# A long convolution's forward Fourier transform: one product over 112 rows against two over 57 and 56 rows of folded sums and differences

## The reference, cut to what matters

```python
# sublayer 1: a state-space layer (B=16, L=112, H=512)
xz = einsum('bld,ed->bel', hidden_states, W_in)
x, z = split(xz, 2, axis=1)                     # 512 channels each
x = silu(conv1d(pad(x), conv_w, depthwise) + conv_b)   # 4 taps, causal
k = _s4d_kernel(...)                            # (512, L), real
n = 2 * L
y = irfft(rfft(x, n=n) * rfft(k, n=n), n=n)[..., :L]
y = (y + x * D) * silu(z)
out = einsum('bhl,dh->bld', y, W_out)
# x1 = layernorm(x + out); sublayer 2 adds x1's projection and a gathered,
# decayed context (layernorm again); sublayer 3 is a mixture of 8 experts,
# one expert for each token (layernorm again)
```

## Time and profile before

| | us |
|---|---|
| median of three runs | 395.71 |
| span of the profiled execution | 390.5 |
| what lies around the span (median less span) | 5.2 |
| stage A, from VectorE's first tap to its last | 25.6 to 60.3 |
| turning point from A to B | 60.3 to 91.5 |
| stage B, steps 3 to 15 | 91.5 to 208.8 |
| stage B, the last steps, and routing | 208.8 to 245 |
| stage F, experts | 245 to 390 |

### The profile page before, as it was taken

The page is one execution under the profiler, slowest core; times in us unless marked ns, Lnnn a source line. Parts: engine busy times, 40 slices in busy tenths (PEclk is TensorE's granted clock), DMA queues, the critical chain, the costliest instruction groups (busy, mean ns, idle before and its releaser), DMA issues.

```text
span 390.5 us, 7319 instructions
## 1 busy us (share of the span) xinstructions
PE 333.8 (85%) x2035; PEld 276.7 (71%) x2036; DVE 249.4 (64%) x491; ACT 124.3 (32%) x332; POOL 225.8 (58%) x390
## 2 busy tenths in 40 slices
PE   2549996789999999999999532799999999999990
PEld 1225544668888887888888422699999999999970
DVE  6997999976887777777776648323443443443431
ACT  2437883541122222222222100144324324334220
POOL 5958994075776767676556502415456556555553
PEclk9957996899999999999999975799999999999996
DMA  7800000243354444444445046401100101001110
GB/s 227 298 0 1 1 0 3 60 136 117 95 155 158 129 151 147 147 134 128 128 128 166 12 176 280 161 2 42 39 29 22 45 27 40 28 20 40 37 37 24
DMA packets 17025, 34.84 MB, mean 89 GB/s; under 512 B 3456, under 2 KB 8455, under 8 KB 16360
## 3 DMA queue, kind: packets, MB, share of 16 engines
q1 hardware_dynamic: 14840, 29.88, 23.8%
q0 software_dynamic: 1872, 4.59, 4.1%
q10 hardware_dynamic: 288, 0.07, 0.1%
HBM read 30.86 MB, written 4.20 MB: 90 GB/s over the span
## 4 chain that ended last, share of the span: by engine, by line
PE 75%; DVE 12%; POOL 4%; issue 4%; ACT 2%; DMA 1%; DVEq 0%; POOLq 0%; ACTq 0%
PE ps L1331 17%; PE ps L1349 15%; PE ps L1200 7%; PE ps L1263 7%; PE ps L1245 6%; PE ps L1147 4%; PE ps L1190 4%; PE ps L1191 4%; PE ps L1283 3%; DVE w L888 2%; DVE w L873 2%; PE ps L1155 1%; PE ps L1287 1%; PE ps L1318 1%; POOL stage_b L583 1%
## 5 line engine op out<-in xcount | busy, mean ns | idle before, releaser
L1331 PEld LDWEIGHTS ps<-stage_b 128*128 128x128 f32 x576 | 68.4, 195 | 2.6 <-DVE stage_b L1096 1.0
L1331 PE MATMUL ps<-stage_b 128*128 128x128 f32 x576 | 68.8, 279 | 1.2 <-ACT stage_b L820 1.2
L1349 PE MATMUL ps<-w,stage_b 128*128 x288 | 65.2, 380 | 0.6 <-DVE stage_b L1121 0.6
L1349 PEld LDWEIGHTS ps<-w,stage_b 128*128 128x128 f32 x288 | 53.3, 190 | 7.5 <-issue 1.0
L603 POOL TENSOR_TENSOR stage_b<-stage_b 112x512 f32<-112x512 f32 x16 | 21.6, 1350 | 42.3 <-DVE stage_b L942 21.7
L925 DVE TENSOR_SCALAR stage_b<-stage_b 112x256 f32<-112x256 f32 (+1 forms) x50 | 20.5, 411 | 35.5 <-POOL stage_b L671 21.8
L811 ACT ACTIVATE stage_b<-ps,b 128x128 f32<-128x128 f32 x144 | 39.2, 384 | 7.2 <-issue 7.2
L942 DVE TENSOR_TENSOR stage_b<-ps,w 112x512 f32<-112x512 f32 x64 | 39.7, 682 | 2.6 <-PE ps L1191 1.3
L643 POOL DMA_INDIRECT stage_b<-x_rows,stage_b x21 | 34.3, 1633 | 10.0 <-issue 6.0
L1200 PEld LDWEIGHTS ps<-w 128*128 128x128 f32 x256 | 32.9, 202 | 8.2 <-issue 6.9
L1096 DVE COPY stage_b<-w 128x2048 f32 x19 | 23.5, 1241 | 19.6 <-issue 14.0
(11 more groups left out here) (156 smaller groups left out, 536.7 us busy)
## 6 DMA issues: line engine op xcount, KB each, us to landing
w<-in_w SPq DMA_DIRECT2D x16, 512.0 KB, 3.9
w<-in_w SPq DMA_DIRECT2D x16, 256.0 KB, 2.9
w<-in_w SPq DMA_DIRECT2D x4, 1024.0 KB, 8.2
stage_b<-in_ctx SPq DMA_DIRECT2D x16, 224.0 KB, 2.9
w<-in_x_t SPq DMA_DIRECT2D x4, 448.0 KB, 5.3
stage_b<-in_x SPq DMA_DIRECT2D x16, 112.0 KB, 2.9
x_rows<-stage_b SPq DMA_DIRECT2D x16, 112.0 KB, 1.9
w<-in_w_in SPq DMA_DIRECT2D x2, 512.0 KB, 6.4
```

What stands on the lines that cost most here:

```text
L1331: last_ = m.matmul(ps[:, 2 * par + f // 4, (f % 4) * P:(f % 4 + 1) * P], w1_now[par][:, k, f * P:(f + 1) * P], rows_t[:, par, k * P:(k + 1 ...
L1349: last_ = m.matmul(ps[:, 4 + par, 0:D], h_t[:, par, f * P:(f + 1) * P], w2[:, e, f, :], start=(f == 0), stop=(f == FT - 1))
```

## The change

Time steps t and 112-t meet the same cosine and the opposite sine, up to a sign that is fixed for even and for odd frequencies. So VectorE makes, for every unit, the sums x[t] + x[112-t] (57 of them) and the differences x[t] - x[112-t] (56 of them), with x[112] taken as zero. They are laid at places 0 to 56 and 64 to 119 (`ODD` = 64, `BINS` = 120) of `folded`, and it is `folded` that TensorE turns. The transform is then one product of rows 0 to 56 and one of rows 64 to 119, both against 120 columns of the constant `fold`, and both again over 512 moving columns. Bank 0 receives the real parts of even frequencies and the imaginary parts of odd ones, bank 1 the others; places 57 to 63 are padding.

Around it: `spec` has four tables of 120 rows for three of 112 (one more product in `kernel_spectrum`, a wider copy L761), and is a tensor of its own. `prod`, `y_spec` and the inverse transform have 120 rows for 112. `turn_kernel` uses bank 3 instead of bank 4. GpSimd clears two small strips at the start. TensorE's turn now waits for `fold_set` instead of `act_x`, and ScalarE's SiLU waits for `fold_set` instead of `xt_ps`. TensorE's 20 steps of stage B are written out instead of partly looped; the other engines keep their loops.

```diff
+HF = L // 2
+ODD = 64
+BINS = ODD + HF
...
-        x_time = r.cut(NB * H, L).rearrange("p (b h) -> p b h", b=NB)
+        x_time = r.cut(NB * H, BINS).rearrange("p (b h) -> p b h", b=NB)
...
@@ GpSimd
+            g.memset(conv_x[:, :, :, L:L + 1], 0.0)
+            g.memset(folded[:, :, :, HF + 1:ODD], 0.0).then_inc(edge_set, 1)
...
@@ ScalarE, a_silu
-                need(act, xt_ps, unit - 1)
-                a.activation(conv_x[:, par, :], conv_acc[:, par, :], ACT.Silu, bias=conv_b[:, h:h + 1])\
+                need(act, fold_set, unit - 1)
+                a.activation(conv_x[:, par, :, 0:L], conv_acc[:, par, :].rearrange("p (b t) -> p b t", b=CB),
+                             ACT.Silu, bias=conv_b[:, h:h + 1])\
...
-                a.activation(spec[:, :, tile], ps[0:L, 5:8, tile], ACT.Copy).then_inc(spec_set, 1)
+                a.activation(spec[:, :, tile], ps[0:BINS, 4:8, tile], ACT.Copy).then_inc(spec_set, 1)
@@ VectorE
+            def a_fold(unit, h):
+
+                x_now, to = conv_x[:, h % 2], folded[:, h % 2]
+                dve.wait_ge(act_x, unit + 1)
+                need(dve, xt_ps, unit - 1)
+                v.tensor_tensor(to[:, :, 0:HF + 1], x_now[:, :, 0:HF + 1], x_now[:, :, L:HF - 1:-1], ALU.add)
+                v.tensor_tensor(to[:, :, ODD:], x_now[:, :, 0:HF], x_now[:, :, L:HF:-1], ALU.subtract)\
+                 .then_inc(fold_set, 1)
...
+            dve.wait_ge(edge_set, 1)
             for h in range(HT):
                 a_step(0, h)
+                if h > 0:
+                    a_fold(h - 1, h - 1)
             with dve.Fori(1, NC) as c:
                 for h in range(HT):
                     a_step(c, h)
+                    a_fold(HT * c + h - 1, (h - 1) % HT)
+            a_fold(HT * NC - 1, HT - 1)
...
-                    for n, (x_part, k_part) in enumerate(((0, 0), (1, 1), (0, 1), (1, 2))):
-                        last = v.tensor_tensor(prod[:, n, :], ps[0:L, x_part, :], spec[:, k_part, :], ALU.mult)
+                    for n in range(4):
+                        last = v.tensor_tensor(prod[:, n, :], ps[0:BINS, n % 2, :], spec[:, n, :], ALU.mult)
@@ TensorE
             def a_turn(unit, h):
-                pe.wait_ge(act_x, unit + 1)
+                pe.wait_ge(fold_set, unit + 1)
                 need(pe, xt_set, unit - 1)
                 for b in range(CB):
-                    last_ = m.transpose(ps[0:L, 4 + h % 2, b * P:(b + 1) * P],
-                                        conv_x[:, h % 2, b * L:(b + 1) * L], ident)
+                    last_ = m.transpose(ps[0:BINS, 4 + h % 2, b * P:(b + 1) * P], folded[:, h % 2, b, :], ident)
...
-                    m.matmul(ps[0:L, 0, :], const("f_re", L), x_time[:, b, :], start=True, stop=True)
-                    m.matmul(ps[0:L, 1, :], const("f_im", L), x_time[:, b, :], start=True, stop=True)\
+                    m.matmul(ps[0:BINS, 0, :], const("fold")[0:HF + 1], x_time[0:HF + 1, b, :], start=True, stop=True)
+                    m.matmul(ps[0:BINS, 1, :], const("fold")[ODD:BINS], x_time[ODD:BINS, b, :], start=True, stop=True)\
...
-                m.transpose(ps[0:L, 4, h * P:(h + 1) * P], kern[:, h, :], ident).then_inc(kern_ps, 1)
+                m.transpose(ps[0:L, 3, h * P:(h + 1) * P], kern[:, h, :], ident).then_inc(kern_ps, 1)
...
-                for s, name in enumerate(("f_re", "f_im0", "f_d")):
-                    last = m.matmul(ps[0:L, 5 + s, tile], const(name, L), kern_t[:, tile], start=True, stop=True)
+                for s, name in enumerate(("k_a", "k_b", "k_c", "k_d")):
+                    last = m.matmul(ps[0:BINS, 4 + s, tile], const(name, L), kern_t[:, tile], start=True, stop=True)
...
-            b_steps(pe, step)
+            for s in range(NB + EPI):
+                step(s // 2, s % 2)
```

More of the change, by code:

```diff
@@ L71, in constant_columns, with bins @@
     put("eps", np.full((P, 1), EPS))
-    angle = 2 * np.pi * np.outer(t, t) / NFFT
-    cos, sin = np.cos(angle), np.sin(angle)
-    nyquist = (-1.0) ** t
-    zero0 = (t > 0).astype(float)
-    put("f_re", cos)
-    f_im = -sin
-    f_im[:, 0] = nyquist
-    put("f_im", f_im)
-    put("f_im0", -sin * zero0)
-    f_d = cos.copy()
-    f_d[:, 0] = nyquist
-    put("f_d", f_d)
-    g_re = 2 * cos / NFFT
-    g_re[0] = 1.0 / NFFT
+    even, odd = 2 * np.arange(HF + 1), 2 * np.arange(HF) + 1
+    def bins(n, f_even, f_odd):
+        a = np.zeros((n, BINS))
+        angle = 2 * np.pi * np.arange(n)[:, None] / NFFT
+        a[:, :HF + 1] = f_even(angle * even)
+        a[:, ODD:] = f_odd(angle * odd)
+        return a
+    minus_sin = lambda v: -np.sin(v)
+    fold = np.zeros((BINS, BINS))
+    fold[:HF + 1] = bins(HF + 1, np.cos, minus_sin)
+    fold[HF] *= 0.5
+    fold[ODD:] = bins(HF, minus_sin, np.cos)
+    put("fold", fold)
+    for name, f_even, f_odd in (("k_a", np.cos, np.sin), ("k_b", np.sin, np.cos),
+                                ("k_c", minus_sin, np.cos), ("k_d", np.cos, minus_sin)):
+        put(name, bins(L, f_even, f_odd))
+    g_re, g_im = 2 / NFFT * bins(L, np.cos, np.cos).T, -2 / NFFT * bins(L, np.sin, np.sin).T
+    g_re[[0, HF]] *= 0.5
     put("g_re", g_re)
-    g_im = -2 * sin / NFFT
-    g_im[0] = nyquist / NFFT
     put("g_im", g_im)
@@ L180, in decoder_layer @@
         conv_acc = r.cut(2 * CW).rearrange("p (r n) -> p r n", r=2)
-        conv_x = r.cut(2 * CW).rearrange("p (r n) -> p r n", r=2)
+        conv_x = r.cut(2 * CB * (L + 1)).rearrange("p (r b t) -> p r b t", r=2, b=CB)
         n_hits = PT * T // 2
@@ L205, in decoder_layer @@
         w_out = r.cut(HT * D).rearrange("p (k d) -> p k d", k=HT)
-        spec = r.cut(3 * H, L).rearrange("p (s h) -> p s h", s=3)
+        folded = r.cut(2 * CB * BINS).rearrange("p (r b t) -> p r b t", r=2, b=CB)
+        spec = sb("spec", [BINS, 4 * H])[:, :].rearrange("p (s h) -> p s h", s=4)
         shared = sb("shared", [P, 2048])
@@ L220, in two @@
             return r.cut(2 * words, rows).rearrange("p (r n) -> p r n", r=2)
-        prod = r.cut(4 * H, L).rearrange("p (s h) -> p s h", s=4)
-        y_spec = r.cut(2 * H, L).rearrange("p (s h) -> p s h", s=2)
+        prod = r.cut(4 * H, BINS).rearrange("p (s h) -> p s h", s=4)
+        y_spec = r.cut(2 * H, BINS).rearrange("p (s h) -> p s h", s=2)
         z_act, gated = two(HT * L), two(HT * L)
@@ L282, in decoder_layer @@
         kern_ps, kern_sb, spec_ps, spec_set = (sem(s) for s in ("kern_ps", "kern_sb", "spec_ps", "spec_set"))
-        in_ps, acc_set, tap_set, conv_done, act_x, xt_ps, xt_set = (
-            sem(s) for s in ("in_ps", "acc_set", "tap_set", "conv_done", "act_x", "xt_ps", "xt_set"))
+        in_ps, acc_set, tap_set, conv_done, act_x, fold_set, edge_set, xt_ps, xt_set = (
+            sem(s) for s in ("in_ps", "acc_set", "tap_set", "conv_done", "act_x", "fold_set", "edge_set", "xt_ps",
+                             "xt_set"))
         dft_ps, prod_set, y_set, z_ps, z_set, idft_ps, gate_set, out_ps = (
@@ L602, in step @@
                     need(pool, idft_ps, b)
-                    g.tensor_tensor(y_spec[:, 0, :], prod[:, 0, :], prod[:, 1, :], ALU.subtract)
+                    g.tensor_tensor(y_spec[:, 0, :], prod[:, 0, :], prod[:, 1, :], ALU.add)
                     g.tensor_tensor(y_spec[:, 1, :], prod[:, 2, :], prod[:, 3, :], ALU.add).then_inc(y_set, 1)
@@ L720, in a_move @@
                 a.activation(x_time[:, bass.ds(CB * c, CB), h * P:(h + 1) * P],
-                             ps[0:L, 4 + h % 2, :].rearrange("p (b h) -> p b h", b=CB), ACT.Copy)\
+                             ps[0:BINS, 4 + h % 2, :].rearrange("p (b h) -> p b h", b=CB), ACT.Copy)\
                  .then_inc(xt_set, 1)
@@ L758, in _ @@
                 act.wait_ge(kern_ps, h + 1)
-                a.activation(kern_t[:, tile], ps[0:L, 4, tile], ACT.Copy).then_inc(kern_sb, 1)
+                a.activation(kern_t[:, tile], ps[0:L, 3, tile], ACT.Copy).then_inc(kern_sb, 1)
                 act.wait_ge(spec_ps, h + 1)
-                a.activation(spec[:, :, tile], ps[0:L, 5:8, tile], ACT.Copy).then_inc(spec_set, 1)
+                a.activation(spec[:, :, tile], ps[0:BINS, 4:8, tile], ACT.Copy).then_inc(spec_set, 1)
             def step(pair, q):
@@ L1245, in step @@
                             last_ = m.matmul(ps[:, 3, h * L:(h + 1) * L], y_spec[:, s, h * P:(h + 1) * P],
-                                             const(name, L), start=(s == 0), stop=(s == 1))
+                                             const(name, BINS), start=(s == 0), stop=(s == 1))
                     last_.then_inc(idft_ps, 1)
```

## The result

The changed kernel takes 406.03 us (median of 4 runs, 404.33 to 406.99), the kernel before in the same series 395.45 us. The ratio is 1.0257, 95% interval 1.0212 to 1.0302: slower, by 10.6 us. The forecast was 412.1 us in a range of 401 to 421.

What follows compares the result with a forecast made beforehand. VectorE was taken to bound stage A's last part and TensorE stage B. Stage A +19.4, the rest +0.5 and stage B -3.5 gave +16.4 us on the profiled execution, 412.1 us, in a range of 401 to 421.

Steps and rivals of the forecast that it cites:

- Part 1: Stage A, VectorE: the folds' own work, 0.32 us each, 0.64 a pair per unit, all on the path.
- Part 2: Stage A: VectorE's folds wait for GpSimd's instructions at the shared port, 1.68 us a pair in 9 units, 0.64 in three.
- Part 3: Edges of stage A: last unit's fold costs 1.4 us, units 0 to 3 cost 1.0; later SiLU wait costs nothing.
- Part 4: Stage B, two forward products on row tiles: 0.43 us overlap less 0.18 transitions, 0.25 a step, 14 steps, -3.5 us.
- Part 5: The rest: TensorE's written-out loop costs and gains nothing; the kernel's spectrum and step 0's transform together +0.5 us.
- port contended, tiles side by side: Rival: folds pay the port in stage A, stage B's products overlap fully; 403.6 us, chance 0.13.
- Free port: Rival: in stage A the port costs nothing for such short folds; 402.8 us, chance 0.17.
- one after the other: Rival: stage B's tiles don't overlap and pay both transitions, 0.18 us a step; 418.1 us, chance 0.12.
- faster: Rival: full overlap in stage B, 0.86 us a step, beside a free port decides; 394.3 us, chance 0.07.
- clock rival: Rival: TensorE, busy for half of stage A's units, falls to 1.2 GHz, +4.0 us; 416.1 us, chance 0.13.

Runs made afterwards that it cites:

- e7: Changed kernel with the folds' second input read from PSUM (folded values left out) and TensorE's turn a unit later: 399.16 us, ratio 1.011.
- e4: Changed kernel with the folds' second input read from PSUM instead of SBUF, folded values left out: 403.09 us, ratio 1.019.
- e6: Changed kernel with GpSimd's 28 products of 256 elements in stage A cut into 56 of 128: 406.54 us, ratio 1.028.
- e12: Changed kernel with TensorE's turn a unit later and the folds placed between the taps, GpSimd's products whole: 401.74 us, ratio 1.014.
- e5: Kernel before the change with only TensorE's loop of stage B written out: 395.67 us, ratio 0.9985.
- e3: Changed kernel with both forward products on rows 0 to 56, one tile, differences left out: step 9.38 us; total 412.19 us, not compared.
- e2: Changed kernel without folds, SiLU writing straight into `folded`, signal's transform left out: first reduction at 58.59 us; total 383.49 us, not compared.
- e1: Changed kernel with both forward products over all 120 rows, so no row tiles, same result: 414.14 us, ratio 1.044.
- e8: Changed kernel with folds' second input from PSUM (folded values left out), turn a unit later, folds between the taps: 401.15 us, ratio 1.016.
- e9: Changed kernel with GpSimd's products halved, the turn a unit later and the folds between the taps, result complete: 401.28 us, ratio 1.019.

## Why the prediction was right, and where it was off

**Direction and size.** Forecast +16.4 us, measured +12.0 on the spans and +10.6 on the medians. The bound engines were read rightly: VectorE in stage A pays, TensorE in stage B gains, and stage F keeps its length (143.7 us from the first expert product on, 143.8 before). The number lay in the range although one step was wrong: the range had been drawn to hold the rivals too, and the two errors below, some 2.4 us in stage A and 2.6 in stage B, both made the forecast too slow.

**Part 1, the folds' own work: right.** Records of 0.38 and 0.39 us where nothing contends, 0.59 a pair in e7 (2.60 less the taps' 2.01), for 0.64.

**Part 2, the port: right in kind, somewhat too dear.** Folds of 0.9 to 1.0 us beside GpSimd and 0.39 after it, units of 3.73 there (61.52 to 65.25) for 3.69 predicted. e4 and e6 show the cause: 8.3 us of the folds' time go when their second input leaves SBUF, and waits shrink with GpSimd's instruction. Too dear, because 8 units paid and not 9, at 3.47 us on the mean (37.50 to 65.25): up to 52 us several first folds found the port free. I had let the folds deny GpSimd 0.64 us a unit and so put its end near 68.7; the end moved from 62.9 to 65.07.

The Trainium skill (SBUF — State Buffer, Who interferes with whom) calls the pair of ports that VectorE and GpSimd share an exclusive lock, and says that a VectorE instruction with two SBUF inputs contends with a GpSimd instruction that reads SBUF. The traces agree: 0.38 us with an input in PSUM, 0.91 with both in SBUF. It doesn't foretell who is next when both wait. The folds and GpSimd's products took turns, and e12's gain rests on that; but e5's L912, with two SBUF inputs of one element each, waited for three products in a row (2.19 us for 0.16), so turns are not a rule.

**Part 3, the edges.** Units 0 to 3 cost 1.5 us (the fifth unit's first tap at 37.50 for 35.99), predicted 1.0. That they came near is luck: the idle 1.84 us that the prediction let the folds fill was a half-clock stretch of TensorE in that one execution, and in e5 the fifth unit starts at 34.33. The last unit cost 1.4 (73.87 to 77.32 less 2.01), as predicted. "SiLU now waits for a fold that is a whole unit older: nothing" held, but I missed its counterpart: TensorE's turn now waits for a fold where it had waited for SiLU, and `a_in` stands behind it. It cost at most 1.1 us in the changed kernel (0.48 of it before the fifth unit, with TensorE at half clock); in e4, without port waits over it, some 2.5 of the 4.5. By stages: 1.5 + 11.5 (eight units) + 2.5 (three) + 1.4, unrounded +17.0, predicted +19.4.

**Part 4, the tiles: the step that failed.** The prediction said: "If starts stay in order, only high1 and low2 can overlap: 0.43 us. I take that". They don't stay in the code's order. The second product's first MATMUL starts 0.01 us after the first product's first, so the four run as two pairs in 1.05 us. In e3, with the same calls in the same order but on one tile, both MATMULs of the first product start before those of the second (128.54 and 129.49), so it is the second tile that lets them pass. The predicted transition of 0.18 us was too low as well, e3 gives 0.29. So 0.85 - 0.29 = 0.56 a step instead of 0.25, and over the 12 steps -6.1 us for 12 x -0.25 = -3.0 (the first of them was shorter than 9.08 before). The range held it (up to 0.86). I had the rule of program order from the Trainium skill (TensorE: Matmul & The Clock Gate, Packing small matmuls). Its short distance between starts agrees with the rows, its order rule doesn't hold for the starts of two float32 products on two row tiles. The Trainium skill also says (TensorEngine Tiling (Array Packing), Key Properties) that a change of tiling mode drains the engine; e3's 0.29 us agree.

A second figure of Part 4: the followers could follow. VectorE has 88.01 of 102.20 us in stage B for 81.39 of 108.40, and TensorE isn't kept waiting. But it is near: of the changed kernel's chain of waits in these steps long parts run through GpSimd's L614, L594 and VectorE's L968 and L984, beside a TensorE without a gap.

**Part 5.** The loop is worth nothing (e5), as predicted. Between the reduction and step 3 the kernel takes 31.15 us for 31.08: the spectrum's +0.5 doesn't show. (e5 and e2 take 33.1 and 33.3, since their first reduction is early and waits for GpSimd.)

**The rivals.** The truest mechanism was one I gave 0.13: port contended, tiles side by side, 403.6 us. It undersold the transitions. "Free port" fell with e4, "one after the other" with e1, "faster" with both. The clock rival, at +4.0 us, fell by the windows: TensorE busy for 3.09 of 6 us and at 1.00. Only between 33 and 37 us did the clock fall again, and VectorE waited 0.48 us for it.

**What stays open.** How GpSimd and VectorE are ordered when both wait was read off timelines, not tried by itself, and L912's three lost turns are unexplained; so are the last steps' 1 to 2 us and the waits in e8. Whether folds on ScalarE or in TensorE's turning product would pay wasn't tried.

## What to carry to other kernels

A fold that halves TensorE's work for one stage is paid on another engine in another stage: price it where that engine is the bound. Here the folds alone cost more (16 x 0.59 us of VectorE; e7, without port waits, reaches step 3 8.4 us later than the kernel before, 1.2 of it its late first fold) than twelve overlapped steps bring (6.1 us). An instruction with two SBUF inputs on VectorE beside a busy GpSimd should stand behind one that reads PSUM, not behind its like: that alone was 4.3 us. And when a signal is moved to a later producer (turn after fold instead of after SiLU), follow the consumer's queue: what is issued behind it waits too. A wait in one profiled execution can be the clock's: look at the granted clock there before an edit is given the credit.

## What the runs showed of the hardware that I had not expected

- Two float32 products on different 64-row tiles interleave by halves: starts at 125.23, 125.24, 125.76, 125.77. A pair takes 0.53 us where one MATMUL of 512 columns alone takes 0.43. In e3 the first and the last of the four take 0.53 and 0.52 us and the two between them 0.43, so the excess stands at the way into the tile and out of it.
- Of two folds beside GpSimd the second waits 0.53 us (0.91 less 0.38) when it follows the first, and not behind a tap of 0.66 us, with GpSimd's products whole. With the halves it has 0.45 us on the mean behind a tap (e9).
- The turns aren't kept always: L912 in e5, 128x1 with both inputs in SBUF, took 2.19 us beside three whole products of GpSimd and 0.16 once they were through.
- Cutting GpSimd's instructions in two shortens VectorE's waits and lengthens GpSimd's work by 4.7 us (25.7 for 21.0): with the folds apart the halves bring 1.2 us at the reduction (71.05 for 72.28) and nothing that the totals can tell (401.28, 401.74).
